# Second attention of a fused decoder: four-row-group score products for the first key block, and a new order of PE's work

## The reference, cut to what matters

```
q = query.reshape(N, Q, 16, 16);  k = key.reshape(N, K, 16, 16);  v = values.reshape(N, K, 16, 16)
energy = einsum('nqhd,nkhd->nhqk', q, k);  energy = where(mask == 0, -1e20, energy)
attn = softmax(energy / sqrt(256), axis=-1)
out = einsum('nhqk,nkhd->nqhd', attn, v).reshape(N, Q, 256) @ W_out.T
```

## Time and profile before

| quantity | value |
|---|---|
| median of three runs | 1359.4 us (1357.12 to 1361.69) |
| the profiled execution's own time | 1359.86 us |
| its span in the trace | 1358.1 us, 1.8 us lie around it |
| PE busy over the span | 1301.9 us, 96% |
| mean granted TensorE clock | 0.986 |
| second attention, first S0 to last O | about 302 to 556 us |

### The profile page before, as it was taken

The page is one execution under the profiler, slowest core; times in us unless marked ns, Lnnn a source line. Parts: engine busy times, 40 slices in busy tenths (PEclk is TensorE's granted clock), DMA queues, the critical chain, the costliest instruction groups (busy, mean ns, idle before and its releaser), DMA issues.

```text
span 1358.1 us, 31988 instructions
## 1 busy us (share of the span) xinstructions
PE 1301.9 (96%) x12737; PEld 996.8 (73%) x12737; DVE 738.9 (54%) x1733; ACT 506.6 (37%) x1074; POOL 288.4 (21%) x384
## 2 busy tenths in 40 slices
PE   7999999999999999799999999999998999999996
PEld 6777887764666666466767998999997667777764
DVE  5666666655666664377754211110113556778886
ACT  2111111112555555356656323232332444444444
POOL 2000000102121221687844000000002001234431
PEclk9999999997999999999999999999998999999999
DMA  7212211012222220022201100000000000000001
GB/s 217 60 44 55 44 32 31 19 30 52 64 59 59 64 50 17 3 61 61 69 14 37 32 1 0 0 3 0 0 0 1 4 5 3 16 17 13 17 7 56
DMA packets 47891, 44.67 MB, mean 33 GB/s; under 512 B 14960, under 2 KB 44448, under 8 KB 47760
## 3 DMA queue, kind: packets, MB, share of 16 engines
q1 hardware_dynamic: 47760, 42.83, 12.2%
HBM read 38.95 MB, written 2.78 MB: 31 GB/s over the span
## 4 chain that ended last, share of the span: by engine, by line
PE 86%; issue 4%; DVE 3%; POOL 2%; ACT 2%; DMA 2%; SPq 1%; DVEq 0%; ACTq 0%; POOLq 0%
PE banks L306 47%; PE banks L790 5%; PE banks L1003 3%; PE banks L941 3%; PE banks L768 3%; PE banks L954 3%; PE banks L806 3%; PE banks L299 3%; PE banks L998 3%; PE banks L935 2%; PE banks L635 2%; PE banks L593 2%; PE banks L982 2%; ACT area L1478 1%; DMA room<-Y_room 1%
## 5 line engine op out<-in xcount | busy, mean ns | idle before, releaser
L1839 DVE TENSOR_REDUCE area<-banks 112x8 f32<-112x896 f32 x96 | 100.2, 1086 | 77.9 <-PE banks L941 77.9
L1734 DVE TENSOR_REDUCE Y_room<-banks 112x2 f32<-112x750 f32 x128 | 114.3, 936 | 47.9 <-PE banks L768 45.9
L1478 ACT ACTIVATE area<-banks 112x896 f32<-112x896 f32 x96 | 82.7, 914 | 120.1 <-PE banks L1003 120.1
L306 PE MATMUL banks<-room,area 128*112 128x256 f32 (+1 forms) x384 | 120.5, 465 | 3.6 <-issue 3.2
L1981 DVE SCALAR_TENSOR_TENSOR X<-banks,area,X 128x192 f32 (+1 forms) x56 | 23.3, 418 | 165.0 <-PE banks L306 165.0
L1374 ACT ACTIVATE area<-banks,Y_room 125x896 f32<-125x896 f32 x96 | 92.3, 1005 | 51.6 <-issue 26.1
L1527 ACT ACTIVATE room<-banks 128x256 f32<-128x256 f32 x123 | 47.1, 383 | 166.1 <-PE banks L306 166.0
L306 PE MATMUL banks<-area,room 128*128 128x224 f32 x512 | 102.9, 360 | 0.6 <-ACT area L1326 0.6
L306 PEld LDWEIGHTS banks<-area,room 128*128 128x128 f32 x512 | 97.3, 193 | 3.1 <-ACT area L1326 1.0
L306 PE MATMUL banks<-room,l 128*128 128x256 f32 x448 | 99.5, 379 | 0.0
L306 PEld LDWEIGHTS banks<-room,area 128*112 128x112 f32 x384 | 67.8, 182 | 40.7 <-issue 27.6
(11 more groups left out here) (240 smaller groups left out, 2508.8 us busy)
## 6 DMA issues: line engine op xcount, KB each, us to landing
area<-den_scratch SPq DMA_DIRECT2D x32, 224.0 KB, 3.8
Y_room<-in_ctx SPq DMA_DIRECT2D x16, 375.0 KB
area<-in_ctxT SPq DMA_DIRECT2D x64, 93.8 KB
l<-in_l SPq DMA_DIRECT2D x2, 1024.0 KB, 5.4
room<-in_ctxT SPq DMA_DIRECT2D x16, 112.0 KB, 2.2
out<-X SPq DMA_DIRECT2D x16, 112.0 KB, 1.9
X<-in_x SPq DMA_DIRECT2D x1, 1568.0 KB, 17.2
room<-in_Wq SPq DMA_DIRECT2D x1, 1024.0 KB, 5.2
```

Source lines behind the costliest of these rows:

```text
L306: last = nc.tensor.matmul(dst, a, w, start=(k == 0), stop=(k == len(lhs) - 1))
L1478: a_.activation(c_pT[:, i * 8 * S:(i + 1) * 8 * S].rearrange("p (j n) -> p j n", j=2), banks[0:S, 2 + 2 * i:4 + 2 * i, 0:4 * S], ACT.Exp). ...
L1734: v_.tensor_reduce(b_nb[u][:, 4 * a + k:4 * a + k + H + 1:H], banks[0:S, 2 * x:2 * x + 2, 0:SC], AX_X, ALU.max, negate=True).then_inc(Bs[" ...
L1839: v_.tensor_reduce(c_nb[:, 8 * i:8 * i + 8].rearrange("q (j n) -> q j n", j=2), banks[0:S, 2 + 2 * i:4 + 2 * i, 0:4 * S].rearrange("q j (n ...
```

## The change

- The first block of keys (c = 0) of both halves of the heads is no longer two lots of four 64-row matmuls with 224 columns. A new function `turned_by_four` (called **F** from here on) makes sixteen matmuls of 18 rows and 112 columns, on four row groups, into two pairs of banks at once. The other four blocks keep their form under the numbers 0, 1, 4 and 5.
- `b_pT` becomes one tile with both halves inside; w2 and w3 write it in a permuted pattern. W01 now needs w0 to w3, W23 also w4 and w5.
- PE's new order in phase b: S0(b), MT(b-1), OT(b-3), T4(b-2), Q(b), T5(b-2), S1(b), W01(b-2), S2(b), W23(b-2), S3(b), U(b-2), T0, T1 and F(b-1), O(b-3).
- ACT's order: copy of MT, copy of OT, w4, the two copies of Q, w5, the copy of the sums, w0 to w3. DVE's order: h0, h1, `queries`, the statistics, h2 to h7, `normalise`, the residual sum.
- The waits that guard bank 7 are rewritten for this order, and `bank_pairs` follows the new order of uses.

```diff
-        for what, n in (("s", 0), ("t", 4), ("t", 5), ("s", 1), ("t", 0), ("t", 1), ("s", 2), ("t", 2), ("t", 3), ("s", 3)):
+        for what, n in (("s", 0), ("t", 4), ("t", 5), ("s", 1), ("s", 2), ("s", 3), ("t", 0), ("t", 1), ("t", 2), ("t", 3)):
...
             def phase_b(b, w, quarter):
-                if on(b - 2):
-                    weighted(b - 2, 0, w % 2)
-                    weighted(b - 2, 1, w % 2)
                 if on(b):
                     scores_b(b, 0, w, quarter)
...
                 if on(b - 1):
+                    maxima_t(b - 1, w - 1)
...
+                if on(b - 3):
+                    output_t(b - 3)
                 if on(b - 2):
                     turned(b - 2, 4, (w - 2) % 4)
+                if on(b + 1):
+                    queries_b(b)
+                if on(b - 2):
                     turned(b - 2, 5, (w - 2) % 4)
...
                 if on(b):
                     scores_b(b, 1, w, quarter)
+                if on(b - 2):
+                    weighted(b - 2, 0, w % 2)
+                    weighted(b - 2, 1, w % 2)
                 if on(b):
                     scores_b(b, 2, w, quarter)
                 if on(b - 2):
                     weighted(b - 2, 2, w % 2)
                     weighted(b - 2, 3, w % 2)
...
                 if on(b):
                     scores_b(b, 3, w, quarter)
+                if on(b - 2):
+                    sums_t(b - 2)
+                if on(b - 1):
+                    turned(b - 1, 0, (w - 1) % 4)
+                    turned(b - 1, 1, (w - 1) % 4)
+                    turned_by_four(b - 1, (w - 1) % 4)
+                if on(b - 3):
+                    output_b(b - 3)
...
+            def turned_by_four(b, w):
+
+                lots = [PAIRS["t", b, n] for n in (2, 3)]
+                for x, need in lots:
+                    freed(need)
+                for k in range(QUAD):
+                    for r in range(4):
+                        o, x = SLOT * r, lots[r // 2][0]
+                        last = T3.matmul(pb[2 * x + r % 2][0:KC, k * S:(k + 1) * S], b_ctx[w][o:o + HD + 2, k, 0:KC],
+                                         b_q[w][o:o + HD + 2, k, r % 2, :], start=True, stop=True)
+                        if k == QUAD - 1 and r % 2 == 1:
+                            last.then_inc(Bs["st"].sem, 1)
...
+LOTS = {0: (0, 1), 1: (0, 2), 4: (1, 1), 5: (1, 2)}
```

More of the change, by code:

```diff
@@ L157, in claim @@
         return x, need
-    for b in range(B + 3):
-        for what, n in (("s", 0), ("t", 4), ("t", 5), ("s", 1), ("t", 0), ("t", 1), ("s", 2), ("t", 2), ("t", 3), ("s", 3)):
+    for b in range(B + 2):
+        for what, n in (("s", 0), ("t", 4), ("t", 5), ("s", 1), ("s", 2), ("s", 3), ("t", 0), ("t", 1), ("t", 2), ("t", 3)):
             if what == "s" and on(b):
@@ L328, in decoder_kernel @@
         b_oT = take(P, KT * S)
-        b_pT = [take(KC, 2 * NKC * QN, "p (c e n) -> p c e n", c=NKC, e=2) for _ in range(2)]
+        b_pT = take(KC, 4 * NKC * QN, "p (c e g n) -> p c e g n", c=NKC, e=2, g=2)
         b_q = [room[:, 2 * i * QN:2 * (i + 1) * QN].rearrange("p (k g s) -> p k g s", k=QUAD, g=2) for i in range(4)]
@@ L695, in queries_b, with maxima_t, output_t, output_b @@
                 last.then_inc(Bs["xq"].sem, 1)
+            def maxima_t(b, w):
+                pe.wait_ge(Bs["nb"].sem, Bs["nb"].at(8 * (b + 1)))
+                pe.wait_ge(Bs["nm"].sem, Bs["nm"].at(b - 1))
+                pe.wait_ge(Bs["xu"].sem, Bs["xu"].at(b - 2))
+                if b < 3:
+                    pe.wait_ge(Bs["qs"].sem, Bs["qs"].at(b + 2))
+                T3.transpose(pb[7][0:2 * H, 2 * P:2 * P + S], b_nb[w % 2], ident[0:S, 0:S]).then_inc(Bs["mt"].sem, 1)
+            def output_t(b):
+                pe.wait_ge(Bs["nm"].sem, Bs["nm"].at(b + 1))
+                transposes(b_o, S, KT, pb[7]).then_inc(Bs["ot"].sem, 1)
+            def output_b(b):
+                pe.wait_ge(Bs["oe"].sem, Bs["oe"].at(b + 1))
+                pe.wait_ge(Bs["nm"].sem, Bs["nm"].at(min(b + 2, B)))
+                if b == 0:
+                    pe.wait_ge(ld["wx"].sem, 16)
+                products(pb[7][0:S, 0:D], [b_oT[:, k * S:(k + 1) * S] for k in range(KT)],
+                         [wx0[:, k, :] for k in range(KT)]).then_inc(Bs["wd"].sem, 1)
+            def sums_t(b):
+                pe.wait_ge(Bs["ue"].sem, Bs["ue"].at(b + 1))
+                pe.wait_ge(Bs["qs"].sem, Bs["qs"].at(min(b + 4, B)))
+                pe.wait_ge(Bs["oe"].sem, Bs["oe"].at(b))
+                pe.wait_ge(Bs["me"].sem, Bs["me"].at(min(b + 2, B)))
+                for t in range(4):
+                    last = T3.transpose(pb[7][0:S, t * P:(t + 1) * P], b_u[:, t * S:(t + 1) * S], ident)
+                last.then_inc(Bs["ut"].sem, 1)
             def phase_b(b, w, quarter):
-                if on(b - 2):
-                    weighted(b - 2, 0, w % 2)
-                    weighted(b - 2, 1, w % 2)
                 if on(b):
                     scores_b(b, 0, w, quarter)
-                pe.wait_ge(Bs["nm"].sem, Bs["nm"].at(b - 2))
                 if on(b - 1):
[L705 to L708, removed]
+                    maxima_t(b - 1, w - 1)
                 if b == 1:
@@ L712, in phase_b @@
                 if on(b - 3):
-                    transposes(b_o, S, KT, pb[7]).then_inc(Bs["ot"].sem, 1)
+                    output_t(b - 3)
                 if on(b - 2):
                     turned(b - 2, 4, (w - 2) % 4)
+                if on(b + 1):
+                    queries_b(b)
+                if on(b - 2):
                     turned(b - 2, 5, (w - 2) % 4)
[L717 to L723, removed]
                 if on(b):
                     scores_b(b, 1, w, quarter)
[L726 to L730, removed]
+                if on(b - 2):
+                    weighted(b - 2, 0, w % 2)
+                    weighted(b - 2, 1, w % 2)
                 if on(b):
@@ L777, in turned @@
             def turned(b, n, w):
-                g, c = divmod(n, NKC)
+                g, c = LOTS[n]
                 if n == 0:
@@ L806, in weighted @@
                         last = T3.matmul(pb[6][32 * j:32 * j + 17, t * S:(t + 1) * S], b_cv[v][:, c, 4 * t + j, :],
-                                         b_pT[g][:, c, j % 2, n * S:(n + 1) * S], start=(c == 0), stop=(c == NKC - 1),
+                                         b_pT[:, c, j % 2, g, n * S:(n + 1) * S], start=(c == 0), stop=(c == NKC - 1),
                                          tile_position=(0, 32 * j))
@@ L1346, in phase_b @@
                     weights(b - 2, 4, w % 2)
[L1347 to L1350, removed]
                 if on(b + 1):
@@ L1358, in phase_b @@
                 if on(b - 2):
+                    weights(b - 2, 5, w % 2)
+                if on(b - 2):
                     act.wait_ge(Bs["pv"].sem, Bs["pv"].at(2 * (b - 1)))
@@ L1362, in phase_b @@
                 if on(b - 1):
-                    weights(b - 1, 2, 1 - w % 2)
-                    weights(b - 1, 3, 1 - w % 2)
+                    for n in range(4):
+                        weights(b - 1, n, 1 - w % 2)
             def weights(b, n, v):
@@ L1369, in weights @@
                     act.wait_ge(Bs["vr"].sem, Bs["vr"].at(b + 1))
-                g, c = divmod(n, NKC)
                 act.wait_ge(Bs["st"].sem, Bs["st"].at(6 * b + n + 1))
-                act.wait_ge(Bs["pv"].sem, Bs["pv"].at(2 * (b - 1) + g + 1))
                 x = PAIRS["t", b, n][0]
-                a_.activation(b_pT[g][:, c, :, :], banks[0:KC, 2 * x:2 * x + 2, 0:QN], ACT.Exp,
-                              bias=b_bias[v][:, c:c + 1]).then_inc(Bs["ex"].sem, 1)
+                if n in LOTS:
+                    g, c = LOTS[n]
+                    act.wait_ge(Bs["pv"].sem, Bs["pv"].at(2 * (b - 1) + g + 1))
+                    a_.activation(b_pT[:, c, :, g, :], banks[0:KC, 2 * x:2 * x + 2, 0:QN], ACT.Exp,
+                                  bias=b_bias[v][:, c:c + 1]).then_inc(Bs["ex"].sem, 1)
+                else:
+                    act.wait_ge(Bs["pv"].sem, Bs["pv"].at(2 * b))
+                    dst = b_pT[:, 0, n - 2, :, :].rearrange("p g (i a s) -> p a (g i) s", i=2, a=2)
+                    a_.activation(dst, banks[0:KC, 2 * x:2 * x + 2, 0:QN].rearrange("p a (k s) -> p a k s", k=QUAD), ACT.Exp,
+                                  bias=b_bias[v][:, 0:1]).then_inc(Bs["ex"].sem, 1)
             act.wait_ge(Bs["ke"].sem, 1)
@@ L1710, in phase_b @@
                     residual_a(B - 1)
[L1711 to L1716, removed]
                 if on(b + 2) and b != -2:
                     stats_of(Bs, b + 2, 1, 0)
+                if on(b):
+                    for n in range(2, 8):
+                        highest(b, n, u)
                 if on(b - 2):
```

15 lines of the change are left out of this document (7 added, 8 removed).

## The result

The changed kernel took 1378.78 us (median of four, 1378.14 to 1388.43) against 1358.54 before: ratio 1.0165, 95% interval 1.0123 to 1.0207, so 1.2 to 2.1% slower. The forecast was slower, 1365, with a range from 1357 to 1374. The direction held, the size did not. The profiled execution took 1378.14 us, its span is 1376.3 against 1358.1.

The account below looks back on a forecast made before the run. Steady phases were taken as PE's work laid end to end, so PE's pieces plus its waits bound the kernel. 1359.86 + 7.8 (twelve phases) - 1.4 (head) + 0 (tail) = 1366.3, stated as 1365 us, range 1357 to 1374.

Parts of the forecast that it names:

- Q's standing still: After S0, MT, OT and T4, PE waits 1.05 us a phase for DVE's `queries`, bounds 0.9 to 1.3.
- F's: 0.45 forecast: After T0 and T1, PE waits 0.45 us a phase until w0 frees F's second pair of banks, bounds 0.2 to 0.7.
- The T0 wait of 0.34: T0's wait for the DMA of the maxima and DVE's reduction, 0.34 us a phase before the change, goes.
- the walk: One steady phase followed from S0's end: period 14.6 us against 13.93, over twelve phases +7.8 us.
- the four terms that I named: Parts of the steady period: 13.06 us of PE work, 1.05 waiting before Q, 0.45 before F, 0.1 before S0.
- F's own price: F's time on PE, taken as 0.98 us from a similar product in a later attention, bounds 0.77 to 1.7.
- the head's term: First phases of the second attention, up to S0(3): 2.7 us earlier if the clock stays up, half taken, -1.4.
- the tail's: From S0(15) to the last O: 38 us against 38.5 before, counted as nothing, bounds -2 to +2.
- the clock's rival: PE's standing still each phase lowers the clock, one slow stretch every third phase: +12, 1377 us; chance 0.16.
- a warm and a cold case: Head with the clock staying up, 2.7 us gained, or falling again, which gives the 2.7 back.
- The 1.3 that I had shaved off my own sum: Sum 1366.3 stated as 1365, because the twelve phases had more bounds downward than upward.
- F's 0.73: F at 0.98 us replaces T lots of 1.71, so PE's work falls 0.73 us a phase.

Follow-up runs that it names:

- experiment 1: Changed kernel with DVE normalising the next batch's rows before h0 and h1 instead of behind them: 1361.73 us, ratio 1.0017 to before.
- experiment 7: Changed kernel with rows normalised before h0 and h1 on DVE, and U moved between T0 and T1: 1358.38 us, ratio 0.9972 to before.
- experiment 4: The order alone: changed kernel with F replaced by two 64-row lots, T2 and T3, behind T1: 1365.93 us, ratio 1.0033 to before.
- experiment 8: The new order with rows normalised before h0 and h1 on DVE and the old 64-row lots, no F: 1352.79 us, ratio 0.9937 to before.
- Experiments 9: The kernel of experiment 7 with F only in batches 2 to 13, 64-row lots in 0, 1, 14 and 15: 1349.90 us, ratio 0.9925 to before.
- experiment 10: Changed kernel with F only in batches 2 to 13, 64-row lots in 0, 1, 14 and 15: 1368.95 us, ratio 1.0063 to before.
- experiment 6: Changed kernel with filler matmuls, three before Q in phases 2 to 14 and eight after O(13): 1374.22 us, ratio 1.0093 to before.
- experiment 2: Changed kernel with Q moved behind S1 on PE and ACT's two copies of Q behind w5: 1363.13 us, ratio 1.0006 to before.

## Why the prediction was wrong

**The waits were right.** Q's standing still: 1.05 forecast, 1.05 in the trace, and Q starts 2.38 after S0's end (2.4 forecast). F's: 0.45 forecast, 0.49. The T0 wait of 0.34 is gone. Experiments 1 and 7 remove them one after the other and the period follows: 14.89, 13.77, 13.42. Nothing else in the walk waited.

**The period was 0.3 short** (14.6 for 14.89): twelve phases were to add 7.8 us and added 11.5, which is 3.7 us of the miss. Some of this is my own sum: the four terms that I named, 13.06, 1.05, 0.45 and 0.1, make 14.66, and 0.73 more than 13.93 would have been +8.8. Of the rest, the largest part is F's own price: 1.14 in the chain, not the 0.98 of the earlier trace rows. That row has 112 weight columns and 32 rows, F has 125 and 18. The rest is some hundredths in F's start, Q and S0. F's price fell within my bounds, but I had argued that the bounds lean down; they leaned up. The Trainium skill ("TensorE: Matmul & The Clock Gate", section Part 2: What happens when you issue a matmul) says that loading weights takes time by their columns. The traces agree: in the timeline a single weight load takes 0.171 us at the median with 18 rows and 112 columns (S, changed kernel), 0.173 with 32 rows and 112 columns (the row, before), and 0.184 with 18 rows and 125 columns (F). An estimate from the columns, 125/112 x 0.98, gives 1.09; the chains show 1.07 where S0 behind it waits little and 1.14 behind F's own wait.

**The step that failed is the head's term, with the tail's and the clock's rival beside it**: they priced PE's waits at full clock, and at the stage's ends the clock fell. I priced the head at -1.4 as the mean of a warm and a cold case; it came out at +1.65, worse than the cold case. Up to MT(1) the walk was right: S0(2) was to end at 334.15, and MT(1) behind it started at 334.01. From there to MT(2) I had 14.65 us, and it took 18.45, at a clock of 0.50 from 334 to 344. I priced the tail at nothing, within 2; it was +3.76. And a further fall of the clock, 2.9 us, sat in the phase after MT(2). I had that as a rival, with 0.16, at "one in every third phase". What came is in between: eleven phases with the 1.05 us gap in each held the full clock, while the ends lost it three times. Sum of the misses, profiled execution against profiled execution: period 3.7, head 3.1, the phase after MT(2) 2.9, tail 3.8, less 1.6 outside the stage, make 11.9 (1378.14 for 1366.3). The 1.3 that I had shaved off my own sum (1366.3 to 1365) went the wrong way and makes it 13.1.

**The sign of F.** I counted F's 0.73 as saved work and its wait of 0.45 as a loss, so as a net gain of 0.3, and it is a net loss of 0.2 in the period (experiment 4 against the changed kernel). Two lots more behind T1 would have cost not 1.71 but 3.22 - 1.71 = 1.51, as the run of four shows; F costs 1.14 plus 0.49, and leaves S0 waiting 0.08. Where nothing waits, F is worth 0.13 a phase (experiment 7's 13.42 against experiment 8's 13.55), not 0.73. The price of what is removed has to be read in the place where it would stand, and I took it from a lone pair.

**F at the ends.** Experiments 9 and 10 take F from batches 0, 1, 14 and 15, and the time falls by 8 and 10 us. In experiment 10 the clock is at 1.00 in both stretches in which it had been at 0.50, and experiment 6 gets back one of them with matmuls that do nothing. In the head this can be divided. Of its 4.3 us between the changed kernel and experiment 10, 4.1 lie between MT(1) and MT(2): 18.45 against 14.37. From Q to U, a stretch in which PE stands still in neither kernel, the changed kernel takes 10.09 us (336.48 to 346.57) and experiment 10 takes 6.53 (336.57 to 343.10): 3.6 us through the clock. From U to MT(2), at full clock in both, it is 5.89 against 5.38: 0.5 us for F and its waits.

The clocks of the timed runs say the same of the executions without a trace. Three of the four runs of the changed kernel had a mean clock of 0.981, all four of experiment 10 had 0.989. A lower mean clock costs at most its own share of the time, since work at half clock took up to twice as long here (a pair of T lots 3.35 for 1.78): 0.008 of 1375 us, an estimate of 11 us at most, where 9.8 were measured. For the order alone (about 0.990) the same estimate gives 12 us at most, beside the 2.4 of the period, where 13 were measured. So nearly all of what F costs beyond the period is consistent with the clock. What makes the clock fall is not shown: it was not tried whether it reacts to F's 18 rows or to the short waits around F, and between MT(2) and MT(3) it kept full speed in experiment 1, which took Q's wait away, and in experiment 10, which took F out of the first batches, but not in experiment 2, where F was there and Q did not wait.

**The tail.** In every kernel with the new order it took 37.7 to 40.5 us against 36.6. In the changed kernel O(13) now stands before the transposes of the next block, and its sum before DVE's chain that feeds them; PE waits there 2.21, F 1.39, and then runs at half clock to 566. I had walked O and its sum, and left out the clock. One piece of it, a pair of T lots that takes 1.78 at full clock:

```profile
561.73 3.35 PE L809 MATMUL banks<-room,area 64*125 64x224 f32 x16
```

From the transposes that end the 2.21 to the U behind them the changed kernel takes 7.86 us (560.82 to 568.68), and experiment 8, with the same order in its tail and full clock, 5.54 (535.25 to 540.79). So 2.3 of the 3.8 us went through the clock.

## What to carry to other kernels

Before moving a step past another on a full engine, ask what its input waits for on the other engines and how long that has been hidden: here 2.4 us from S0 to Q were covered by 6.1 us of PE's work (407.31 to 413.39) and then by 1.3. A product that fills two buffers at once at its end saves matmul time and takes it back if a reader frees them one at a time; here it paid only after another step had been put into the gap (period 13.42, against 13.55 without it), and not in the first and last batches of the pipeline. Where short gaps are added, price the ends of the stage by themselves: here the clock fell there and not in between.

## What the runs showed of the hardware

- Groups of matmuls of one form in a row are cheaper than the same ones split: a lone lot of 448 columns took 0.95 to 0.98, in a pair 0.855, in a run of four 0.805. Two more lots cost 3.22 - 1.71 = 1.51, so 0.755 each, and what is left is 0.20 for each start of a row of lots. The Trainium skill ("TensorEngine Tiling (Array Packing)", section Tiling Modes, Key Properties) says that a change of tiling mode drains TensorE; the steps agree in kind, but no run here tells the drain from any other cost of a start.
- PE stood still for 1.05 us and 0.49 us in each of eleven phases at a granted clock of 1.00 (busy 141.83 of the 158 us from 372 to 530). The clock fell at 334, after waits of 0.25 and 0.39 us, at 354.5, after waits of 0.49, 0.44 and 1.05, of which the steady phases have the first and the last too, and near 559, after 1.39 and within the wait of 2.21. The rule that I had weighed, that short idles between groups can make the clock swing, is that of the Trainium skill ("TensorE: Matmul & The Clock Gate", section A second HAM failure mode); the traces agree with it at the ends of this stage and not inside it, and what decides between the two is not shown.
